# Batch 1's attention keys: masks and heads made inside the last two experts, remainders on GpSimd between later queries

## The reference, cut to what matters

```
energy = einsum('nqhd,nkhd->nhqk', q, k)          # k = ctx, 16 heads of 16
energy = where(mask == 0, -1e20, energy)
attn   = softmax(energy / sqrt(256), axis=-1)
out    = einsum('nhqk,nkhd->nqhd', attn, v) @ W_out.T
```

## Time and profile before

| what | value |
|---|---|
| time, median of 3 runs | 760.51 us (758.94 to 761.31) |
| the profiled execution's own time | 759.17 us |
| its span in the trace | 757.3 us |
| PE busy | 640.5 us, 85% of the span |
| DVE busy | 622.8 us, 82% |
| ACT busy | 530.3 us, 70% |
| POOL busy | 308.1 us, 41% |
| mean granted PE clock | 0.93 |

### The profile page before, as it was taken

How to read it: one execution, slowest core, us unless ns; L and a number is a source line. 1 busy time by engine, 2 the same in 40 slices (tenths; PEclk the granted TensorE clock), 3 DMA queues, 4 the chain that set the end, 5 groups by cost and what they waited for, 6 DMA issues and landing times.

```text
span 757.3 us, 12157 instructions
## 1 busy us (share of the span) xinstructions
PE 640.5 (85%) x4243; PEld 385.4 (51%) x4243; DVE 622.8 (82%) x1304; ACT 530.3 (70%) x713; POOL 308.1 (41%) x249
## 2 busy tenths in 40 slices
PE   6983038999999789999999999999998996029998
PEld 5762024666555544466455645644443444006887
DVE  5898897998999699886887877989897999995433
ACT  2134564777675648888998996666657996996873
POOL 4336603477777627360343120014412443892000
PEclk9997559999999999999999999999999999559999
DMA  9945664466753580000041001021102413101443
GB/s 300 321 152 200 208 169 142 120 146 166 190 134 56 89 289 1 1 23 1 1 149 34 1 29 40 18 83 56 56 0 112 167 55 112 56 0 56 147 133 112
DMA packets 59542, 78.17 MB, mean 103 GB/s; under 512 B 7904, under 2 KB 48224, under 8 KB 59488
## 3 DMA queue, kind: packets, MB, share of 16 engines
q1 hardware_dynamic: 49936, 60.58, 24.4%
q0 software_dynamic: 7872, 14.82, 9.0%
q10 hardware_dynamic: 1680, 2.08, 0.8%
HBM read 50.07 MB, written 27.39 MB: 102 GB/s over the span
## 4 chain that ended last, share of the span: by engine, by line
PE 58%; DVE 16%; ACT 10%; POOL 3%; issue 2%; DMA 1%; POOLq 0%; DVEq 0%
PE bank L2569 10%; PE bank L2303 8%; PE bank L2247 8%; PE bank L2601 5%; PE bank L1584 4%; PE bank L1641 4%; PE bank L1626 3%; PE bank L1694 3%; DVE above L850 2%; PE bank L1656 2%; DVE qx L1307 2%; ACT wgateT L2196 2%; PE bank L1599 2%; PE bank L1665 2%; PE bank L1621 2%
## 5 line engine op out<-in xcount | busy, mean ns | idle before, releaser
L1307 DVE TENSOR_REDUCE qx<-bank 128x4 f16<-128x616 f32 x128 | 98.0, 801 | 22.1 <-PE bank L1584 20.4
L1440 ACT ACTIVATE x<-bank,bic 128x512 f32<-128x512 f32 x160 | 104.6, 690 | 15.9 <-PE bank L1626 12.1
L2247 PE MATMUL bank<-ux,uwh 128*128 128x512 f16 x384 | 92.7, 384 | 0.0
L2247 PEld LDWEIGHTS bank<-ux,uwh 128*128 128x128 f16 x384 | 38.0, 99 | 46.8 <-issue 2.8
L1584 PE MATMUL bank<-Kb,qTb 128*128 128x308 bf16 x256 | 52.5, 297 | 2.0 <-DVE qx L1307 1.1
L2247 PE MATMUL bank<-ux,uwl 128*128 128x512 f16 x192 | 49.9, 383 | 0.0
L1232 POOL CAST qx<-q 128x1024 f16<-128x1024 f32 x8 | 8.5, 1066 | 98.3 <-PE bank L1599 87.3
L1626 PE MATMUL bank<-qT,K 128*128 128x512 f16 x128 | 44.4, 380 | 0.3
L2303 PE MATMUL bank<-uwh,oh 128*128 128x256 f16 x192 | 44.1, 276 | 0.0
L2303 PE MATMUL bank<-uwl,oh 128*128 128x256 f16 x192 | 44.1, 275 | 0.0
L2254 PE MATMUL bank<-uwh 128*128 128x512 f16 x39 | 12.9, 501 | 36.1 <-DVE peak L1977 36.1
(11 more groups left out here) (459 smaller groups left out, 1876.0 us busy)
## 6 DMA issues: line engine op xcount, KB each, us to landing
x_dram<-x SPq DMA_DIRECT2D x4, 1024.0 KB, 5.3
xr<-in_w1T SPq DMA_DIRECT2D x8, 512.0 KB, 3.8
xr<-in_w3T SPq DMA_DIRECT2D x8, 512.0 KB, 4.9
xr<-in_w2T SPq DMA_DIRECT2D x8, 512.0 KB, 6.4
row_dram<-xn SPq DMA_DIRECT2D x8, 512.0 KB, 3.0
x_dram<-xr SPq DMA_DIRECT2D x8, 512.0 KB, 3.0
x<-x_dram SPq DMA_DIRECT2D x8, 512.0 KB, 4.7
xT<-in_xT SPq DMA_DIRECT2D x7, 512.0 KB, 7.8
```

The source lines that it names most:

```text
L1307: dve.tensor_reduce(qx[:, k, g * GH:(g + 1) * GH, MROW].rearrange("p (u h) -> p u h", u=2), pair[i][:].rearrange("p (u x) -> p u x", u=2)[ ...
L1440: act.activation(dst, S_[u % 2], ACT.Exp, bias=bic[:, s // 2, int(tail):int(tail) + 1], scale=1.0 / 16).then_inc(p_done, 1)
L2247: mm = pe.matmul(bank[j][:, m * TB:(m + 1) * TB], w[:, c * HI + cols:c * HI + cols + P], x[:, part, c * TB:(c + 1) * TB], start=(w is uwh ...
```

## The change

Batch 1's keys are no longer made at the start of the attention.

- **Masks.** DVE makes mask 0 in expert 6, between the lower half of the rows (`rows_lo`) and `yw`; mask 1 in expert 7 after `h_lo(2)`; masks 2 and 3 in expert 7 between the second and the third, and the third and the fourth `yw`.
- **Heads.** ACT makes them in expert 7. Each 64x1024 head becomes two of 64x512 (`key_head`). Three of them go between `gate` and `hh` of c = 0, 1, 2; the two 64x104 of the first half go after `hh` of c = 0 and 1; the rest goes after the last `hh`.
- **Remainders.** POOL makes them after the queries of block 2 and before `split(2)` (`key_remainders_gpsimd`). DVE's one instruction (multiply, subtract) becomes two: one multiplication of all of `raw[0]` in place (128x1232), then six subtractions of 16x1024 and 16x104, each behind a wait for the one before.

```diff
+        def key_remainders_gpsimd(pool, raw, K, Kr, b):
+            pool.wait_ge(k_hi, NKH * (b + 1))
+            pool.wait_ge(q_q, 3 * QT)
+            pool.tensor_scalar(raw[0][:], raw[0][:], any16[:, b:b + 1], None, ALU.mult).then_inc(k_raw, 1)
+            pool.wait_ge(k_raw, 1)
+            for h in range(2):
+                rows = slice(h * SW + 32, h * SW + 48)
+                made = NKH * b + 3 * h
+                if h:
+                    pool.wait_ge(k_lo, made)
+                pool.tensor_tensor(K[rows, :, h, :], raw[0][rows, :, 0:P], K[rows, :, h, :], ALU.subtract).then_inc(k_lo, 1)
+                for a in range(2):
+                    pool.wait_ge(k_lo, made + 1 + a)
+                    pool.tensor_tensor(key_tail(Kr, rows, h, a), raw_tail(raw[0], rows, a), key_tail(Kr, rows, h, a), ALU.subtract).then_inc(k_lo, 1)
+            pool.wait_ge(k_lo, NKH * (b + 1))
...
                     queries(s)
+                    if s == 2:
+                        key_remainders_gpsimd(pool, raw, K[1], Kr[1], 1)
                     split(s)
...
-                keys(1, "mask")
-                keys(1, "remainders")
...
-                for h in range(2):
-                    key_heads(act, raw, K[1], Kr[1], 1, h)
...
+                            if c == 2 and not more:
+                                key_mask(1)
...
+                        if more == 1:
+                            key_mask(0)
...
                             for k in range(CT):
+                                if k >= 2:
+                                    key_mask(k)
                                 dve.wait_ge(e_y, e + 3 + k)
...
+                            if not more and c < 3:
+                                key_head(act, raw, K[1], 1, c // 2, c % 2)
                             h_hi(e, c)
+                            if not more and c < 2:
+                                key_tail_head(act, raw, Kr[1], 1, 0, c)
+                        if not more:
+                            key_head(act, raw, K[1], 1, 1, 1)
+                            for a in range(2):
+                                key_tail_head(act, raw, Kr[1], 1, 1, a)
```

More of the change, by code:

```diff
@@ L275, in build @@
         identb, identr = sb(resid, "identb", [P, P], BF16), halves(resid, "identr", [P, P])
-        k_in, k_set, k_kb, k_hi, k_lo, w_in = (sem("key_" + n) for n in "in set kb hi lo w".split())
+        k_in, k_set, k_kb, k_hi, k_lo, w_in, k_raw = (sem("key_" + n) for n in "in set kb hi lo w raw".split())
         g_mask, g_mk = sem("g_mask"), sem("g_mk")
@@ L287, in raw_tail, with masked_key @@
             return kraw[rows, 4 * a:4 * a + 4, P:S2]
+        def masked_key(dve, raw, Kb, b, j):
+            dve.wait_ge(k_in, 32 * (b + 1))
+            rows = slice(j * MW, (j + 1) * MW)
+            dve.tensor_tensor(Kb[rows, :, j, :], raw[1][rows], kbm[rows, b:b + 1, :].broadcast_to([MW, G, S2]), ALU.mult).then_inc(k_kb, 1)
         def masked_keys(dve, raw, Kb, b):
-            dve.wait_ge(k_in, 32 * (b + 1))
             for j in range(GH):
-                rows = slice(j * MW, (j + 1) * MW)
-                dve.tensor_tensor(Kb[rows, :, j, :], raw[1][rows], kbm[rows, b:b + 1, :].broadcast_to([MW, G, S2]), ALU.mult).then_inc(k_kb, 1)
+                masked_key(dve, raw, Kb, b, j)
         def key_heads(act, raw, K, Kr, b, h):
@@ L300, in key_heads, with key_head, key_tail_head @@
                 act.activation(key_tail(Kr, rows, h, a), raw_tail(raw[0], rows, a), ACT.Copy, scale=any16[rows, b:b + 1]).then_inc(k_hi, 1)
+        def key_head(act, raw, K, b, h, part):
+            rows, pairs = slice(h * SW, (h + 1) * SW), slice(part * PR // 2, (part + 1) * PR // 2)
+            act.wait_ge(k_in, 32 * (b + 1))
+            head = act.activation(K[rows, pairs, h, :], raw[0][rows, pairs, 0:P], ACT.Copy, scale=any16[rows, b:b + 1])
+            if part:
+                head.then_inc(k_hi, 1)
+        def key_tail_head(act, raw, Kr, b, h, a):
+            rows = slice(h * SW, (h + 1) * SW)
+            act.activation(key_tail(Kr, rows, h, a), raw_tail(raw[0], rows, a), ACT.Copy, scale=any16[rows, b:b + 1]).then_inc(k_hi, 1)
+        def key_remainders_gpsimd(pool, raw, K, Kr, b):
[13 more added lines that the diff above has]
+            pool.wait_ge(k_lo, NKH * (b + 1))
         def key_remainders(dve, raw, K, Kr, b, h):
@@ L2401, in h_lo, with key_mask @@
                         dve.tensor_tensor(hl[:, c, :], h[:, c, :], hh[:, c, :], ALU.subtract).then_inc(e_hl, 1)
+                    def key_mask(j):
+                        dve.wait_ge(k_set, 4)
+                        masked_key(dve, raw, Kb[1], 1, j)
                     def block_scales(e):
```

## The result

The changed kernel takes 762.2 us (median of 20 runs, 759.47 to 764.11); the kernel before takes 760.45 us beside it (median of 20 runs). The ratio is 1.002, 95% interval 1.0011 to 1.0029: slower by about 1.75 us by the medians, 0.8 to 2.2 us by the interval. The prediction was 763.0, within 759.8 to 765.6, with +2.7 us as its sum.

The account below looks back on a forecast made before the run. PE was taken to bound the attention, the last expert's transfers and DRAM its start. 759.17 + 0 + 0 + 2.7 = 761.9; the runs' median being 1.3 higher gave 763.2, stated as 763.0, range 759.8 to 765.6.

Parts of the forecast that it names:

- The hidden work: Start of the attention: removing 6.9 us of DVE work and 3.4 us of ACT work is worth 0.
- Masks and heads in the experts: Experts 6 and 7: masks and heads fit the gaps, the third and fourth `yw` about 0.2 us late; cost 0.
- The indirect transfers: Last expert's transfers on POOL: third 0.46 us less, perhaps 0.4 more from mask 2; 0 net, bounds -0.5 and +0.5.
- earlier first statistics: Start of the attention: DVE's first statistics stay at about 266; coming earlier would show the prediction wrong.
- POOL's length: After block 2's queries: POOL's remainders take 8.6 us, 300.22 to 308.8, so `split(2)` isn't late.
- Far from 1.35 us: POOL's multiplication of 128x1232: taken as 1.35 us; a time far from that would show the prediction wrong.
- What it does to DVE: Norm pieces of blocks 3 and 4 wait for POOL's subtractions, delaying PE's unit at 305.78; +2.7 us, bounds 0 and +5.5.
- Loads: Batch 2's raw keys, issued at about 308.8, land at 318 before masks at 328.57; slack 10 us, cost 0.
- Given back: PE's waits after 312, pieces of 0.2 us: some vanish because ACT has caught up, giving back some tenths.
- The first: Unit at 305.78: DVE's waits don't reach PE, not slower; 760.5, with the transfers' bound 760.0; chance 0.23.
- The second: POOL's multiplication is slow, at L1246's rate: DVE loses up to 5.5 us, 766.0, or about 764.5 between; chance 0.12.
- The third and fourth: Third: a gap in expert 7 is too small, 764.0, chance 0.06. Fourth: removed work was worth something, 758 or less, 0.06.

Follow-up runs that it names:

- before with POOL remainders: Kernel before with one part of the change alone, the remainders on GpSimd after block 2's queries; ratio 1.0019 to the kernel before.
- memsets: Changed kernel with batch 1's remainders left out and eight GpSimd memsets of 128x1232 at the same point; ratio 1.0005 to the kernel before.
- the split halves: Changed kernel with multiplication and first half's three subtractions at the attention's start, second half's after block 2's queries; ratio 0.9996 to the kernel before.

## Why the prediction was right

**The hidden work.** Right. Removing 6.9 us from DVE and 3.4 from ACT at the start was worth nothing: DVE's idle time before the statistics grew from 2.94 to 8.97 us.

**Masks and heads in the experts.** Right at 0: ratio 1.0001 with only these in place. Mask 0 fills its gap, with 0.42 us left; the third and fourth `yw` come 0.3 to 0.4 us late, not 0.2. PE's transposes and ACT's L1525 (L1498 before) start 0.4 us late with them, and behind the wait for the rows nothing of it is left.

**The indirect transfers.** The mechanism was right and the place half right. I had mask 2 stretch the first transfer; it was mask 3 that stretched the second. First issue to end of the fourth went from 7.63 to 7.48 us, inside the bounds of 0.5 each way. One of my signs of being wrong, earlier first statistics, came in part: they follow the first issue after 12.17 us instead of 12.54, little more than the two traces with the same code differ (12.54 and 12.25). The Trainium skill's reading (SBUF — State Buffer, "Who interferes with whom"), gave 0 for this term; the runs show a stretch, but only where a mask was well under way when the transfer began, and about 0.1 us shorter than what was left of that mask (0.47 us left, 0.35 longer, in the changed kernel; 0.62 left, 0.5 longer, in before with POOL remainders; 0.1 left, none). What in the transfer waits, no run here shows.

**POOL's length.** 302.66 to 312.18 is 9.5 us against 8.6, and `split(2)` wasn't late. Inside the sum the multiplication was mis-sized: 3.41 us where I took 1.35 from L1925. "Far from 1.35 us" was one of my own signs of being wrong, and for this term it came true. The row was the wrong one by its form, not its types: L1925 isn't one multiplication, as I wrote, but has a second one by 1.0. Written like that, it takes 1.29. A second operation alone doesn't make it fast, though: L1246 has two, a subtraction and a multiplication with a column each, and takes 1.22 us for 256 elements. Which part of its form costs that, no run here separates. The other terms were nearer: 2.05 for 2.2, 0.37 for 0.38 (the slope that I named gives 0.34), and 0.08 for 0.17 between POOL's own instructions.

**What it does to DVE.** This is the step that carried the forecast, and the mechanism holds in every test: two-operand pieces wait to the end of a POOL subtraction (1.11, 1.91, 2.11 and 1.92 us in four places), and not beside memsets. I had called all pieces two-operand; L206 has one, and waited as well (1.72). As the same page of the Trainium skill says it, the two exclude each other for a whole instruction; the trace agrees for the subtractions, down to 0.05 us. For the multiplication it agrees less well: L200, issued in its midst, ended at 305.73, and L201 and L202 ran in 0.16 us each, all before its recorded end at 306.07 (0.34 us early; 0.35 in before with POOL remainders). My prediction said that this rule speaks against the part; it speaks for the cost. The size was off: +2.7 forecast, +1.70 in the hole. The longer multiplication moved the first large subtraction 2.0 us later than in my schedule and the second 1.6, so that L200 lost 0.6 us instead of 1.3 and all of L206 to L212 fell behind one large subtraction instead of meeting two. PE's unit came 1.6 us late instead of 2.8 to 3.2.

**Loads.** Right. Batch 2's raw keys land 4.2 us after their issue at 312.6, not 9.0, and the masks that need them start at 332.52.

**Given back.** I took off some tenths; nothing is given back: from the first statistics it is +1.75 to `split(2)` and +1.73 to `split(7)`.

**The rivals.** The first (the waits don't reach PE) is refuted by the trace for this kernel, and made true by the split halves. The second had half a point: the multiplication was slow. But I had priced 2.7 us of it at 764.5 and more of it dearer, and at 3.41 us the kernel takes 762.2; against the form that takes 1.29 the hole is 0.48 us shorter, not longer. I had taken it that a longer multiplication costs DVE more, and that is the part of my reasoning that the runs refute at this length. The third and fourth didn't come.

## What to carry to other kernels

Before work goes to an idle GpSimd, list what VectorE does in that hole: instructions with two SBUF operands waited here for a GpSimd subtraction to its end, however small they were (128x8 for up to 2.1 us), and a chain of dependent ones can pay for several in turn. Length is a poor measure of that cost; position decides (9.5 us of POOL work in one place cost 1.73 us up to `split(7)`, the same work in two better places 0.12). Look at all of the other engine's instructions around the place, old ones too, before moving anything out of the way.

## What was unexpected of the hardware

- `tensor_scalar` on GpSimd, f32 to f32, 128x1232: 3.41 us with one operation, 1.29 us with a second one that multiplies by 1.0.
- A one-input `tensor_scalar` on VectorE (128x8 int32) took 0.78 and 0.43 us beside GpSimd memsets, where two-operand instructions took 0.16.
- GpSimd's indirect transfers (`yw` to `x2_dram`) took 1.55 to 1.57 us alone, and those of the last two experts 1.79 to 2.10 when a VectorE instruction with two SBUF operands was well under way as they began. In the loop before, where such instructions follow one another, they took up to 2.75.
